# A graph layer's edge pass: picks of v and bf16 parts written with two-tensor VectorE operations

## The chip, the cores and the metric

The kernel runs on one core of a Trainium2 chip. The metric is the device time of one execution in microseconds (us). A core has five engines that run side by side and meet only at semaphores: TensorE (PE, with its weight loads as PEld), VectorE (DVE), ScalarE (ACT), GpSimd (POOL) and SyncE (SP), which only starts DMAs here. SBUF is the on-chip memory of 128 partitions, PSUM the small memory that PE writes to.

## The reference

A message passing layer over 6250 nodes with 64 features and 100000 edges (src, dst), the edges sorted by dst. `basis` holds 8 numbers for each edge.

```python
h = jnp.maximum(_layernorm(x, axis=-1), 0.0)
p1 = jnp.tanh(p @ pp_W1 + pp_b1) @ pp_W2 + pp_b2        # p = h
inter = jnp.concatenate([p1[idx_i], p1[idx_j]], axis=-1)  # idx_i = src, idx_j = dst
inter = inter @ pi_W1 + pi_b1
inter = inter @ pi_W2 + pi_b2
inter = inter @ pi_W3
inter = inter.reshape(inter.shape[0], D, N_BASIS)
i1 = jnp.einsum('ecb,eb->ec', inter, basis)
i1 = jnp.tanh(i1 @ ii_W1 + ii_b1) @ ii_W2 + ii_b2
out = jax.ops.segment_sum(i1, idx_j, num_segments=p1.shape[0])
return x + out
```

## The kernel before

A first stage of some 65 us works on the nodes. It normalises x, applies the first layers and multiplies the weights that stand between the gather and the einsum into each other, so that an edge needs only a row u[src] and a row v[dst] and their sum. The rows go to two tables in DRAM: `u_tab` in fp32, `v_tab` as three bf16 parts whose sum is the value.

The main stage goes over 391 groups of 512 edges (four tiles of 128, `TILES`, `GE`). Each engine has its own program, with the steps of successive groups interleaved: in step n, DVE works for groups n−4 to n+1. The order is written out by hand, and the engines meet at counting semaphores.

- POOL (L444 to L457) gathers the u rows: for each group four indirect DMAs (L453) with 128 rows each. An indirect DMA reads its 128 row numbers from `src_e` in SBUF. `u_rows` has UR = 8 buffers, so POOL waits (`s_ready`) only for the group eight before.
- SP (L367 to L391) brings for each group `loc_bc`, the place of each of the 512 destinations within a window of W = 42 nodes, spread to 126 partitions, and `v_win`, the window's 42 rows of v in three parts.
- DVE makes from them the pick `hot_t` (L834, `pick_t`): a bf16 0/1 matrix, 126 x 512, that is 1 where the place of the edge is the partition's number in `iota_p`. PE multiplies `v_win` by it (L1101, `sum_v`) and so picks the row of v of each edge, and adds the gathered rows of u in the same PSUM bank by a product with the identity (L1109, `place_rows`), which sets `s_ready`.
- ACT copies the sum to `st_sb` (L601). PE spreads the basis numbers over the features (L1118). DVE multiplies the two (L769, `products`, from SBUF and PSUM into `o_sb`), PE contracts (L1126), ACT takes tanh (L589), PE turns the result (L1133), ACT copies (L592), PE sums by destination (L1193) with the 0/1 matrix `hot` that DVE makes at L887 from two SBUF tensors, and DVE adds the sums of the window to `acc_all` (L862).
- Every 16 groups (`PIECE`) DVE splits the basis numbers of the next 16 into three bf16 parts, in steps of their own: `split_first` (L795, a rounding copy from fp32 to bf16), `split_less` (L799, subtract), `split_second` (L804, a rounding copy of the rest) and `split_third` (L808, subtract). Each works on 128 x 512 elements, all in SBUF. Every four groups it transposes the parts (L817, `turn`).

DVE's order within a step is: L862, then in some steps one of the four split operations, then in every fourth step L817, then the pick L834 for group n+1, then L887 for group n−2, then L769 for group n−1. Before the loop, DVE makes the parts of the first piece and the first pick. `zero1` is a column of zeros, 128 x 1, fp32, and `iota_p` a column with each partition's number within its third of the 126, fp32.

In the listing, the `Else` branches are for destination lists that don't fit the windows; they are not taken with these inputs.

Of the kernel before, what the change touches and what calls it, by code (L numbers as in the profile page):

```python
# [8 lines left out]
def program(nc, x, src, dst, edge_attr, pp_W1, pp_b1, pp_W2, pp_b2, pi_W1, pi_b1, pi_W2, pi_b2, pi_W3,  # L9
            ii_W1, ii_b1, ii_W2, ii_b2, out, u_tab, v_tab, loc_tab):  # L10
    f32, i32, u32, bf16 = mybir.dt.float32, mybir.dt.int32, mybir.dt.uint32, mybir.dt.bfloat16
    ALU, ACT, AX = mybir.AluOpType, mybir.ActivationFunctionType, mybir.AxisListType

    N, D = x.shape
    E, NB = edge_attr.shape
    P = 128
# [16 lines left out]
    TILES = 4  # L33
    GE = P * TILES
# [5 lines left out]
    W = P // 3  # L40
# [9 lines left out]
    VR = 4  # L50
# [24 lines left out]
    with ctx:  # L75
        def sb(name, shape, dt=f32):
            return ctx.enter_context(nc.sbuf_tensor(name, shape, dt))

        def sem(name):
            return ctx.enter_context(nc.semaphore(name))  # L80
# [16 lines left out]
        iota_p = sb("iota_p", [P, 3])  # L97
# [10 lines left out]
        loc_bc = sb("loc_bc", [P, VR, GE], bf16)  # L108
        hot_t = sb("hot_t", [3 * W, 2, GE], bf16)
# [36 lines left out]
        zero1 = sb("zero1", [P, 1])  # L146
# [68 lines left out]
        part1 = sem("part1_")  # L215
        part1r = sem("part1r")
        part2 = sem("part2_")
        part3 = sem("part3_")
        loc_ready = sem("loc_ready")
        hot_t_ready = sem("hot_t_ready")  # L220
# [41 lines left out]
        def ld_count(k):  # L262

            return 32 * (k // LD + 1)
# [369 lines left out]
        def _(dve):  # L634
# [141 lines left out]
            def span_of(k):  # L776
                return min(PIECE, NG - k * PIECE)

            def parts_of(k):
                return b_parts[:, k % 2 * PIECE:k % 2 * PIECE + span_of(k), :, :]  # L780

            def rest_of(k):
                return b_rest[:, 0:span_of(k), :, :]

            def basis_of(k):
                return basis[:, k * PIECE * NBT:(k * PIECE + span_of(k)) * NBT].rearrange(
                    "p (g t b) -> p g t b", t=TILES, b=NB)

            def split_first(k):
                dve.wait_ge(ld[k % LD], ld_count(k))  # L790
                if k == PIECES - 1:
                    dve.wait_ge(last_in, 32)
                if k >= 2:
                    dve.wait_ge(turned, (k - 1) * (PIECE // BT))
                nc.vector.tensor_copy(parts_of(k)[:, :, :, 0:NB], basis_of(k)).then_inc(part1, 1)  # L795

            def split_less(k):
                dve.wait_ge(part1, k + 1)
# [2 lines left out]

            def split_second(k):
                dve.wait_ge(part1r, k + 1)
                nc.vector.tensor_copy(parts_of(k)[:, :, :, NB:2 * NB], rest_of(k)).then_inc(part2, 1)  # L804

            def split_third(k):
                dve.wait_ge(part2, k + 1)
# [22 lines left out]
            def pick_t(g):  # L830
                dve.wait_ge(loc_in[g % VR], 16 * (g // VR + 1))
                if g >= 2:
                    dve.wait_ge(s_ready, g - 1)
                nc.vector.tensor_scalar(hot_t[:, g % 2, :], loc_bc[0:3 * W, g % VR, :], iota_p[0:3 * W, 0:1], None,  # L834
                                        ALU.is_equal).then_inc(hot_t_ready, 1)

            def add_early(b):
                cols = slice(slices_of(b).start * D, slices_of(b).stop * D)
# [3 lines left out]

            with dve.If(is_fast):
                split_first(0)
                split_less(0)
                split_second(0)
                split_third(0)
                turn(0)
                places()
                pick_t(0)  # L850
                for n in STEPS:
                    if n == 4:
                        dve.wait_ge(acc_zero, 1)
                    if has(n - 4):
                        g = n - 4
# [11 lines left out]
                    k = n // PIECE + 1  # L867
                    if k < PIECES:
                        if n % PIECE == 6:
                            split_first(k)  # L870
                        if n % PIECE == 8:
                            split_less(k)
                        if n % PIECE == 10:
                            split_second(k)
                        if n % PIECE == 12:
                            split_third(k)
                    if n % BT == 2 and has(n + 2):
                        turn((n + 2) // BT)
                    if has(n + 1):
                        pick_t(n + 1)  # L880
                    if has(n - 2):
                        g = n - 2
# [9 lines left out]
                    if has(n - 1):  # L892
                        g = n - 1
# [370 lines left out]
```

## Time and profile before

| | us |
|---|---|
| median of 3 runs | 2033.84 |
| lowest and highest of them | 2032.79, 2038.43 |
| the profiled execution | 2041.94 |
| its span in the trace | 2039.9 |

| engine | busy us | share of the span | instructions |
|---|---|---|---|
| PE | 1756.2 | 86% | 19956 |
| PEld | 1145.7 | 56% | 19956 |
| DVE | 1325.6 | 65% | 1894 |
| ACT | 1099.3 | 54% | 2401 |
| POOL | 1506.6 | 74% | 1582 |

All rows come from the one profiled execution; its own time is 2041.94 us, a little above the three others. A group row gives an operation's line, engine, name, the tile written and the tiles read, the shapes, its count, its busy time and mean, and the idle time of the engine just before such instructions with what ended most of it. "issue" is idle time in which the engine waited for nothing that the profile shows. In the timeline a row is an instruction or several alike: start, duration, engine, line, operation, tiles. The starts of two DVE instructions that follow each other directly overlap by some 0.08 us in these records.

### The profile page before, as it was taken

The numbers are of one execution on the slowest core, as the hardware profiler recorded it, in microseconds if no ns is written. First come the engines' busy times: TensorE is split into PE (matmuls) and PEld (weight loads), VectorE is DVE, ScalarE is ACT, GpSimd is POOL, SyncE is SP. The second block draws the span as 40 slices with busy tenths as digits, with TensorE's granted clock in tenths as the row PEclk, the third lists the DMA queues.
The fourth block names the chain that finished last, engine by engine and source line by source line (L and its number), as shares of the span: only waits on it lengthen the run. The fifth ranks groups of instructions, "written<-read, shape, count | busy, mean of one in ns | idle before, by whom it ended". The sixth has DMA issues, their size and how long they took to land.

```text
span 2039.9 us, 54797 instructions
## 1 busy us (share of the span) xinstructions
PE 1756.2 (86%) x19956; PEld 1145.7 (56%) x19956; DVE 1325.6 (65%) x1894; ACT 1099.3 (54%) x2401; POOL 1506.6 (74%) x1582
## 2 busy tenths in 40 slices
PE   5698888888889888888888988989888888888988
PEld 4465555555555555555555555555555555555765
DVE  6676666666666666666666666666666666666665
ACT  4565555555555555555555555555555555555554
POOL 2777777777777777777777777777777777777774
PEclk9799999999999999999999999899999998998999
DMA  5533233222332332322323323323233233222231
GB/s 124 132 68 62 54 62 61 56 60 55 60 61 55 61 62 55 63 58 58 60 55 60 61 55 62 60 55 61 55 61 60 55 60 61 55 57 55 58 73 40
DMA packets 261682, 126.82 MB, mean 62 GB/s; under 512 B 183545, under 2 KB 233704, under 8 KB 261432
## 3 DMA queue, kind: packets, MB, share of 16 engines
q1 hardware_dynamic: 210915, 74.15, 17.1%
q0 software_dynamic: 50048, 51.35, 12.8%
q14 instruction: 102, 0.84, 0.1%
q8 instruction: 23, 0.38, 0.1%
q10 hardware_dynamic: 594, 0.10, 0.0%
HBM read 119.47 MB, written 6.00 MB: 62 GB/s over the span
## 4 chain that ended last, share of the span: by engine, by line
POOL 68%; issue 22%; PE 6%; DMA 2%; DVE 1%; SPq 1%; ACT 0%; DVEq 0%; ACTq 0%; POOLq 0%
POOL u_rows L453 68%; PE bank L1126 3%; PE bank L1109 1%; DMA u_rows<-u_tab,src_e 1%; PE bank L1193 1%; PE bank L1133 0%; PE spread_ps L1118 0%; DMA x_sb<-x 0%; DMA v_tab<-acc_all 0%; PE bank L1101 0%; PE spread_ps L988 0%; PE spread_ps L976 0%; ACT loc_rows L557 0%; SPq L340 0%; DMA loc_bc<-loc_tab 0%
## 5 line engine op out<-in xcount | busy, mean ns | idle before, releaser
L453 POOL DMA_INDIRECT u_rows<-u_tab,src_e x1564 | 1500.1, 959 | 509.2 <-issue 474.5
L769 DVE TENSOR_TENSOR o_sb<-st_sb,spread_ps 128x2048 f32<-128x2048 f32 x391 | 894.1, 2287 | 488.9 <-PE spread_ps L1118 485.5
L601 ACT ACTIVATE st_sb<-bank,s_bias 64x256 f32<-64x256 f32 x1564 | 734.2, 469 | 473.8 <-PE bank L1109 457.3
L1126 PE MATMUL bank<-o_sb,g_sb 128*64 128x256 f32 x6256 | 837.7, 414 | 0.8 <-ACT t_sb L592 0.8
L1126 PEld LDWEIGHTS bank<-o_sb,g_sb 128*64 128x64 f32 x6256 | 444.4, 146 | 243.7 <-issue 55.9
L1109 PE MATMUL bank<-ident,u_rows 128*128 128x128 f32 x1564 | 285.6, 306 | 231.1 <-DMA u_rows<-u_tab,src_e 230.2
L1109 PEld LDWEIGHTS bank<-ident,u_rows 128*128 128x128 f32 x1564 | 209.2, 194 | 279.4 <-DMA u_rows<-u_tab,src_e 258.7
L1193 PEld LDWEIGHTS bank<-hot,t_sb 128*65 128x65 f32 x3128 | 225.3, 144 | 158.2 <-issue 155.9
L589 ACT ACTIVATE tt_sb<-bank,z_bias 128x256 f32<-128x256 f32 x391 | 185.5, 474 | 204.5 <-PE bank L1126 204.5
L1193 PE MATMUL bank<-hot,t_sb 128*65 128x42 f32 x3128 | 272.6, 240 | 0.5 <-ACT t_sb L592 0.5
L592 ACT COPY t_sb<-bank 128x256 f32<-128x256 f32 x391 | 146.8, 376 | 221.1 <-PE bank L1133 221.1
L862 DVE TENSOR_TENSOR acc_all<-acc_all,bank 65x42 f32 x391 | 76.4, 195 | 189.0 <-PE bank L1193 184.4
L1133 PE MATMUL bank<-ident,tt_sb 128*128 128x128 f32 x782 | 172.5, 303 | 0.6 <-ACT tt_sb L589 0.6
L1118 PE MATMUL spread_ps<-bt_sb,spread 24*128 24x128 bf16 x6256 | 162.1, 222 | 0.6 <-DVE o_sb L769 0.6
L834 DVE TENSOR_SCALAR hot_t<-loc_bc,iota_p 126x512 bf16<-126x512 bf16 x391 | 141.0, 361 | 10.8 <-DMA loc_bc<-loc_tab 9.4
L1101 PE MATMUL bank<-hot_t,v_win 126*64 126x128 bf16 x1564 | 118.6, 231 | 23.6 <-DVE hot_t L834 15.4
L887 DVE TENSOR_TENSOR hot<-loc_e,iota_f 128x168 f32<-128x168 f32 x391 | 126.9, 325 | 0.1
L1118 PEld LDWEIGHTS spread_ps<-bt_sb,spread 24*128 24x128 bf16 x6256 | 93.0, 94 | 49.7 <-issue 4.0
L1101 PEld LDWEIGHTS bank<-hot_t,v_win 126*64 126x64 bf16 x1564 | 55.5, 108 | 92.8 <-issue 90.8
L1133 PEld LDWEIGHTS bank<-ident,tt_sb 128*128 128x128 f32 x782 | 82.9, 147 | 33.9 <-ACT tt_sb L589 1.4
L817 DVE STREAM_TRANSPOSE bt_sb<-b_parts 128x512 bf16<-128x512 bf16 x98 | 68.8, 702 | 0.3 <-issue 0.3
L1141 PEld LDWEIGHTS bank<-w_out,acc_all 65*64 65x64 f32 (+1 forms) x160 | 15.9, 247 | 2.0 <-issue 0.4
(111 smaller groups left out, 223.2 us busy)
## 6 DMA issues: line engine op xcount, KB each, us to landing
loc_bc<-loc_tab SPq DMA_DIRECT2D x391, 126.0 KB
u_rows<-u_tab,src_e POOLq DMA_INDIRECT x1564
v_win<-v_tab SPq DMA_DIRECT2D x391, 15.8 KB
basis<-edge_attr SPq DMA_DIRECT2D x24, 256.0 KB, 4.0
v_tab<-acc_all SPq DMA_DIRECT2D x6, 336.0 KB
u_tab<-basis SPq DMA_DIRECT2D x6, 224.0 KB
x_sb<-x SPq DMA_DIRECT2D x1, 1120.0 KB
out<-x_sb SPq DMA_DIRECT2D x1, 784.0 KB
```

The source lines that it names most:

```text
L453: pool.indirect_dma_start(out=u_rows[:, g % UR, j, :], out_offset=None, in_=u_tab[:, :], in_offset=bass.IndirectOffsetOnAxis(ap=src_e[:, g ...
L589: return nc.scalar.activation(tt_sb[:, r, :], z_ps, ACT.Tanh, bias=z_bias[:, 0:1])
L592: return nc.scalar.copy(t_sb[:, r, :, 0:D].rearrange("p (h q) c -> p q h c", h=2), t_ps.rearrange("p (q h c) -> p q h c", q=2, h=2))
L601: last = nc.scalar.activation(tiles[h * D:(h + 1) * D, j], s_ps[r][part].rearrange("p (q a e) -> p q a e", q=2, a=TILES), ACT.Identity, bi ...
L769: return nc.vector.tensor_tensor(o_sb[:, r, :, :].rearrange("p c (j e) -> p j c e", j=TILES), st_sb[:, r, :].rearrange("p (j e) -> p j e", ...
L834: nc.vector.tensor_scalar(hot_t[:, g % 2, :], loc_bc[0:3 * W, g % VR, :], iota_p[0:3 * W, 0:1], None, ALU.is_equal).then_inc(hot_t_ready, 1)
L1101: nc.tensor.matmul(s_ps[u % 2][TWICE[j], q * P:(q + 1) * P].rearrange("k (a e) -> k a e", a=TILES), v_win[:, u % VR, :], hot_t[:, u % 2, : ...
L1109: last = nc.tensor.matmul(s_ps[r][:, q * P:(q + 1) * P], rows[:, 2 * q:2 * q + 2, :].rearrange("p j k -> p (j k)"), ident[:], start=alone ...
L1118: last = nc.tensor.matmul(spread_ps[:, a, c * P:(c + 1) * P], spread[q, 2 * c:2 * c + 2, :].rearrange("p b k -> p (b k)"), bt_sb[q, r, :], ...
L1126: last = nc.tensor.matmul(z_ps[h * D:(h + 1) * D, 0:2 * P], g_sb[:, c, :], o_sb[:, r, c, 2 * h * P:(2 * h + 2) * P], start=(c == 0), stop= ...
L1133: last = nc.tensor.transpose(t_ps[:, q * P:(q + 1) * P], tt_sb[:, r, q * P:(q + 1) * P], ident[:])
L1193: last = nc.tensor.matmul(seg_ps, t_sb[:, (u - 3) % 2, j, :], hot[:, (u - 3) % HR, j, :], start=(j == 0), stop=(j == TILES - 1))
```

## The change

The pick, L834, is a comparison of a tensor with a column as a per-partition scalar (`tensor_scalar`). It becomes a comparison of two tensors, the second being the same column repeated along the 512 elements (`tensor_tensor`). The two rounding copies of the split, L795 and L804, become sums of the same input with the column `zero1` repeated over its elements, written to the same bf16 places. Values, shapes, semaphores and the order of the work stay as they are. The copy in the branch that isn't taken stays too.

```diff
--- before.py
+++ after.py
@@ -786,13 +786,18 @@
                 return basis[:, k * PIECE * NBT:(k * PIECE + span_of(k)) * NBT].rearrange(
                     "p (g t b) -> p g t b", t=TILES, b=NB)
 
+            def rounded(to, of, n):
+
+                zero = zero1[:, 0:1].unsqueeze(2).unsqueeze(3).to_broadcast([P, n, TILES, NB])
+                return nc.vector.tensor_tensor(to, of, zero, ALU.add)
+
             def split_first(k):
                 dve.wait_ge(ld[k % LD], ld_count(k))
                 if k == PIECES - 1:
                     dve.wait_ge(last_in, 32)
                 if k >= 2:
                     dve.wait_ge(turned, (k - 1) * (PIECE // BT))
-                nc.vector.tensor_copy(parts_of(k)[:, :, :, 0:NB], basis_of(k)).then_inc(part1, 1)
+                rounded(parts_of(k)[:, :, :, 0:NB], basis_of(k), span_of(k)).then_inc(part1, 1)
 
             def split_less(k):
                 dve.wait_ge(part1, k + 1)
@@ -801,7 +806,7 @@
 
             def split_second(k):
                 dve.wait_ge(part1r, k + 1)
-                nc.vector.tensor_copy(parts_of(k)[:, :, :, NB:2 * NB], rest_of(k)).then_inc(part2, 1)
+                rounded(parts_of(k)[:, :, :, NB:2 * NB], rest_of(k), span_of(k)).then_inc(part2, 1)
 
             def split_third(k):
                 dve.wait_ge(part2, k + 1)
@@ -831,8 +836,9 @@
                 dve.wait_ge(loc_in[g % VR], 16 * (g // VR + 1))
                 if g >= 2:
                     dve.wait_ge(s_ready, g - 1)
-                nc.vector.tensor_scalar(hot_t[:, g % 2, :], loc_bc[0:3 * W, g % VR, :], iota_p[0:3 * W, 0:1], None,
-                                        ALU.is_equal).then_inc(hot_t_ready, 1)
+                nc.vector.tensor_tensor(hot_t[:, g % 2, :], loc_bc[0:3 * W, g % VR, :],
+                                        iota_p[0:3 * W, 0:1].to_broadcast([3 * W, GE]), ALU.is_equal
+                                        ).then_inc(hot_t_ready, 1)
 
             def add_early(b):
                 cols = slice(slices_of(b).start * D, slices_of(b).stop * D)
```

## Rows read from the trace of the kernel before

**Rows 1.** The page: busy time of each engine; the chain that ended last.

```profile
PE 1756.2 (86%) x19956; PEld 1145.7 (56%) x19956; DVE 1325.6 (65%) x1894; ACT 1099.3 (54%) x2401; POOL 1506.6 (74%) x1582
...
POOL 68%; issue 22%; PE 6%; DMA 2%; DVE 1%; SPq 1%; ACT 0%; DVEq 0%; ACTq 0%; POOLq 0%
POOL u_rows L453 68%; PE bank L1126 3%; PE bank L1109 1%; DMA u_rows<-u_tab,src_e 1%; PE bank L1193 1%; PE bank L1133 0%; PE spread_ps L1118 0%; DMA x_sb<-x 0%; DMA v_tab<-acc_all 0%; PE bank L1101 0%; PE spread_ps L988 0%; PE spread_ps L976 0%; ACT loc_rows L557 0%; SPq L340 0%; DMA loc_bc<-loc_tab 0%
```

**Rows 2.** Line L453: the page's row, then durations and what POOL idled for.

```profile
L453 POOL DMA_INDIRECT u_rows<-u_tab,src_e x1564 | 1500.1, 959 | 509.2 <-issue 474.5
...
L453 POOL DMA_INDIRECT u_rows<-u_tab,src_e x1564: 941/947/1528, 40.2 to 2016.0; - x196
...
  issue: 474.5, 1556
...
  PE bank L1109: 2.1, 7
```

**Rows 3.** The page: L769 and L834; then from the waits: PE for the gather.

```profile
L769 DVE TENSOR_TENSOR o_sb<-st_sb,spread_ps 128x2048 f32<-128x2048 f32 x391 | 894.1, 2287 | 488.9 <-PE spread_ps L1118 485.5
L834 DVE TENSOR_SCALAR hot_t<-loc_bc,iota_p 126x512 bf16<-126x512 bf16 x391 | 141.0, 361 | 10.8 <-DMA loc_bc<-loc_tab 9.4
...
PE bank L1109 <- DMA u_rows<-u_tab,src_e: 230.2, 152, 2.9
```

**Rows 4.** Timeline, DVE and POOL: start us, us, engine, line, operation, tiles, idle before.

```profile
998.83 2.29 DVE L769 TENSOR_TENSOR o_sb<-st_sb,spread_ps 128x2048 f32<-128x2048 f32 x1 [0.87 <-PE spread_ps L1118]
999.83 0.94 POOL L453 DMA_INDIRECT u_rows<-u_tab,src_e  x1 [0.30 <-issue]
1001.08 0.95 POOL L453 DMA_INDIRECT u_rows<-u_tab,src_e  x1 [0.31 <-issue]
```

**Rows 5.** Timeline, POOL and DVE, from 410.5 us.

```profile
410.59 1.53 POOL L453 DMA_INDIRECT u_rows<-u_tab,src_e  x1 [0.30 <-issue]
410.62 0.68 DVE L799 TENSOR_TENSOR b_rest<-basis,b_parts 128x512 f32<-128x512 f32 x1
```

**Rows 6.** Timeline, POOL and DVE, from 1228.1 us.

```profile
1228.11 1.26 POOL L453 DMA_INDIRECT u_rows<-u_tab,src_e  x1 [0.30 <-issue]
1228.14 0.42 DVE L804 CAST b_parts<-b_rest 128x512 bf16<-128x512 f32 x1
```

**Rows 7.** Timeline, DVE and POOL, from 152.9 us.

```profile
152.98 0.35 DVE L834 TENSOR_SCALAR hot_t<-loc_bc,iota_p 126x512 bf16<-126x512 bf16 x1
153.10 1.05 POOL L453 DMA_INDIRECT u_rows<-u_tab,src_e  x1 [0.31 <-issue]
```

**Rows 8.** Timeline, DVE and POOL, from 800.3 us.

```profile
800.32 0.33 DVE L887 TENSOR_TENSOR hot<-loc_e,iota_f 128x168 f32<-128x168 f32 x1
800.35 1.12 POOL L453 DMA_INDIRECT u_rows<-u_tab,src_e  x1 [0.30 <-issue]
```

**Rows 9.** Timeline, DVE and POOL, from 1403.1 us.

```profile
1403.17 0.68 DVE L808 TENSOR_TENSOR b_parts<-b_rest,b_parts 128x512 bf16<-128x512 f32 x1
1403.77 0.34 DVE L834 TENSOR_SCALAR hot_t<-loc_bc,iota_p 126x512 bf16<-126x512 bf16 x1
1403.81 1.37 POOL L453 DMA_INDIRECT u_rows<-u_tab,src_e  x1 [0.30 <-issue]
1404.03 0.32 DVE L887 TENSOR_TENSOR hot<-loc_e,iota_f 128x168 f32<-128x168 f32 x1
```

**Rows 10.** Timeline, DVE and POOL, from 835.2 us.

```profile
835.28 0.68 DVE L808 TENSOR_TENSOR b_parts<-b_rest,b_parts 128x512 bf16<-128x512 f32 x1
835.78 1.00 POOL L453 DMA_INDIRECT u_rows<-u_tab,src_e  x1 [0.30 <-issue]
```

**Rows 11.** Groups by shape, DVE: columns as on the page.

```profile
L799 DVE TENSOR_TENSOR b_rest<-basis,b_parts 128x512 f32<-128x512 f32 x24 | 16.4, 681 | 0.0
```

**Rows 12.** Timeline, PE, the rows of u placed by two successive groups.

```profile
83.17 0.71 PE L1109 MATMUL bank<-ident,u_rows 128*128 128x128 f32 x4
...
87.27 0.71 PE L1109 MATMUL bank<-ident,u_rows 128*128 128x128 f32 x4
```

## The prediction

> **What bounds the kernel now.** I read the page first, then the group rows, then the order of time around single instructions, because the change touches small VectorE operations and the question is whom they hold up. PE is busiest by share, 86%, but the chain that ended last runs 68% on POOL's line L453 and 22% in "issue", the pause between two POOL instructions [rows 1]. L453 is the gather of rows of u: 1564 indirect DMAs, four for each of the 391 groups [rows 2]. POOL's idle time before them is almost all "issue" (1556 times, 474.5 of 509.2 us), and the waits for PE are 2.1 us [rows 2]; the rest is one wait before the first gather. So POOL never really waits for a consumer: it goes from the first gather at 40.2 us to the last at 2016.0 us without a stop, and the other engines follow it. PE waits for u_rows 152 times, 230.2 us, and VectorE sits idle 488.9 us before its big product L769 [rows 3]. That is the cover of VectorE: 1.25 us a group.
>
> An undisturbed gather takes 0.95 us and starts 1.25 us after the one before [rows 4]. 1563 steps of 1.25 us are 1954 us; the trace has 2016.0 − 40.2 = 1975.8 us. So about 20 us are lost in gathers that take longer. The same number comes from the group: 1500.1 us busy less 1564 × 0.947 us (the median) is 19.0 us, with single gathers up to 1.53 us [rows 2]. I looked for what runs beside the long ones.
>
> **What a VectorE instruction does to a gather.** At 410.59 us the gather took 1.53 us: L799, a tensor_tensor whose two inputs both lie in SBUF, ran from 410.62 for 0.68 us, to 410.59 + 0.71. The excess is 1.53 − 0.95 = 0.58 us, which is L799's end less 0.13 us [rows 5]. At 1228.11 the cast L804 ended 0.45 us after the gather's start and the gather was 0.31 us too long: its end less 0.14 [rows 6]. At 153.10 the pick of v, L834, ended 0.23 after the start and the excess was 0.10 [rows 7]. At 800.35 it was L887, again a tensor_tensor from two SBUF tensors: end at 0.30, excess 0.17 [rows 8]. So each of these four kinds holds the gather back, if it runs at the gather's start, until the operation's end; the gather then goes on, 0.13 us of its own being done. Work with one input in PSUM does not show this: L769 runs over gather starts in every group, and those gathers take 0.94 to 0.95 us, as the two at 999.83 and 1001.08 [rows 4]. Whether the operation is a one-input cast or a two-input tensor_tensor decides nothing; its length does.
>
> **A price per operation.** If an operation of length d can catch a start from its own first moment up to 0.13 us before its end, and starts fall every 1.25 us at any phase, its mean cost is w²/2/1.25 with w = d − 0.10 (casts, L799, L808: the latest that still caught a gather began 0.03 us after it [rows 5, 6]). The pick must wait for two semaphores and gets hold later; of picks with no split operation ahead of them I found none that caught a gather after beginning less than 0.06 us before it, so w = d − 0.20. L887 has w of 0.16. Checked against the trace of now: L834, d 0.35: 0.009 × 391 = 3.5 us; L887: 0.010 × 391 = 4.0; the 50 casts, d 0.42: 0.041 × 50 = 2.0; L799 and L808, d 0.68: 0.135 × 49 = 6.6. Sum 16 us against the 19 to 20 measured. The rest is a second kind: at 1403.81 the gather was 0.42 us too long with L834 ending at 0.30 and L887 at 0.54, that is L887's end less 0.12. Behind the long L808 both were ready, and L887 went ahead of the waiting gather [rows 9]. The opposite is there too: at 835.78 the excess was only 0.05, L808's end at 0.18 less 0.13, and the gather slipped in ahead of L834 [rows 10].
>
> **The change, part by part.** It moves nothing: the same instructions stand in the same order on every engine, with the same waits.
>
> (a) The pick, 391 times, becomes a tensor_tensor of 512 elements a partition, bf16 against an fp32 column spread with step 0. The nearest row is L799, a 128x512 tensor_tensor of mixed types, 681 ns; L834 is 361 ns [rows 3, 11]. VectorE gets 391 × 0.32 = 125 us more work. All of it lies in the 488.9 us of cover; if the cover were gone it would cost its 125 us. Who waits for the pick: behind it on VectorE L887 and L769, on PE sum_v of the next group. PE can make a step in 4.10 us when rows are there (83.17 to 87.27 [rows 12]) while POOL needs 1975.8 / 391 = 5.05 us a group, so 0.3 us of lateness in a step is caught up. Cost on the path by time alone: 0.
> By holding gathers: w grows from 0.15 to 0.48; 0.48²/2.5 = 0.092 us × 391 = 36 us, less the 3.5 of now: +32.5 us.
>
> (b) The first halves of the split: 50 casts of 0.42 us [rows 6] become sums of 0.68 us. VectorE +12 us, under the same cover. Holding: 0.135 × 50 = 6.7, less 2.0: +4.7 us.
>
> (c) L887 right behind the longer pick. In a 0.68 us pick there is time to get L887 ready, and both are now the same kind of operation. If L887 always waits its turn behind the gather, as L834 did at 835.78, nothing is added. If it goes ahead as at 1403.81 once the pick has run 0.25 us, a gather caught in the later part waits for L887's end, 0.25 us more: (0.21 × 0.375 + 0.52²/2)/1.25 = 0.171 us a group for both, against 0.092 + 0.012 = 0.104 apart; +26 us, and up to some 12 us more behind the 49 operations L799 and L808. Bounds 0 and +38. I take +21, near the middle, because the two rows that bear on it point opposite ways.
>
> Sum: 32.5 + 4.7 + 21 = +58 us. Each microsecond here is on POOL's own chain and nothing can hide it. The tail after the last gather has no picks; the prologue has two casts more of 0.25 us while POOL already runs ahead: 0.
>
> Here a rule of the Trainium skill stands against my reading. "SBUF — State Buffer", section "Who interferes with whom", says that copies, casts and tensor_scalar can take two port pairs and then lock GpSimd out fully, while tensor_tensor has no such mode, touches only GpSimd's reads, and did not stall DMAs in their probe because descriptor writing needs the write side (marked as inferred there). By it the change would give back what the picks and casts cost, a sum of −8 us in place of +58. The trace disagrees in the point that matters: the longest gather of all, 1.53 us, stood beside a tensor_tensor [rows 5].
>
> **Against the runs.** The profiled execution took 2041.94 us (span 2039.9), the median of the three is 2033.84 us. The sum is a difference against that execution; phases alone can move its 20 us by several, so I add it to the median: 2033.84 + 58 = 2092 us.
>
> **The rivals.**
> *The new operations don't hold gathers (faster).* Then the 3.5 + 2.0 us, and the 3 us of the second kind, vanish: −8 us, 2026 us. It decides if a step-0 second input is not such a read. Against it: L887 has step-0 inputs and holds gathers [rows 8]. Chance 0.04.
> *The phases don't mix.* If VectorE's steps settle at a phase to the gathers, the pick could miss nearly all starts, costing some 0 to 6 us net (chance 0.03, no change), or hit most, at up to 0.48 us a group: far over +100. Now the picks fall at all phases, and PE's catching up in every second or third group stirs them. Most of it lies above the range (0.05 there), less of it between 2040 and 2052 us (0.04).
> *L887 never goes ahead*: +37 us, 2071. *It always does*, with the chains: +75, 2109. Both inside the forecast.
> *VectorE becomes the bound.* It needs 1325.6 + 137 = 1463 us of 2100, 3.7 us a group; it would have to pass 5.05 us a group. Under 0.01.
>
> **Numbers.** A measurement of this kernel tells 0.3%, 6 us, from no change. The forecast case runs from L887 never to L887 always ahead, 2071 to 2109 us. The rule gave 16 us where the trace had 20, so a quarter of its new total (16 + 58 − 21 = 53 at the one end, 91 at the other) may be luck of the phases: 2071 − 19 (the quarter of 53 and 6 us between the runs themselves) and 2109 + 23, which is 2052 to 2132 us. It has 0.84; slower but outside it 0.09; same 0.03; faster 0.04. So faster 0.04, same 0.03, slower 0.93, and the predicted time is 2092 us.
>
> **What would show it.** Right: the pick and the sums at 0.68 us; L453 still 1564 times with a median of 0.947 us but a mean of about 0.996 (0.959 + 58/1564), with hundreds of gathers of 1.1 to 1.7 us; POOL's idle time still "issue"; VectorE near 1463 us busy and L769's idle time down by some 80 us. Wrong: if the mean stays at 0.96 or falls, two-input picks hold nothing and step (a) falls; if POOL starts to wait for L1109, the cover was too thin; if the mean is over 1.03, the phases lock.

## The result, and the profile after

The changed kernel takes 2101.32 us (median of 4 runs, 2099.01 to 2109.22), the kernel before 2036.13 us in its 4 runs. The ratio is 1.0322, with a 95% interval of 1.0305 to 1.0339: slower by 65 us.

The page of the kernel after, its engines, its chain and the four groups that matter. L839 is now the pick (before L834), L893 the making of `hot` (before L887), L868 the adding of the window (before L862), L804 and L813 the two subtractions of the split (before L799 and L808), and L792 the new sum with zero.

```profile
PE 1775.3 (85%) x19956; PEld 1156.6 (55%) x19956; DVE 1456.5 (69%) x1894; ACT 1100.3 (52%) x2401; POOL 1565.5 (75%) x1582
...
POOL 72%; issue 22%; PE 3%; DMA 1%; DVE 0%; SPq 0%; DVEq 0%; ACT 0%; POOLq 0%
...
L453 POOL DMA_INDIRECT u_rows<-u_tab,src_e x1564 | 1559.0, 997 | 510.6 <-issue 474.8
L769 DVE TENSOR_TENSOR o_sb<-st_sb,spread_ps 128x2048 f32<-128x2048 f32 x391 | 893.9, 2286 | 417.9 <-PE spread_ps L1124 406.9
...
L839 DVE TENSOR_TENSOR hot_t<-loc_bc,iota_p 126x512 bf16<-126x512 bf16 x391 | 263.9, 675 | 10.2 <-DMA loc_bc<-loc_tab 8.9
L893 DVE TENSOR_TENSOR hot<-loc_e,iota_f 128x168 f32<-128x168 f32 x391 | 127.3, 325 | 0.0
```

Against [rows 1 to 3], POOL is busy 58.9 us longer, 1559.0 in L453 after 1500.1, and the span has grown by 59.4 (2099.3 after 2039.9). L453's mean went from 959 to 997 ns at the same count of 1564. The time in which POOL stood before L453 is the same, 510.6 after 509.2, and again "issue". So the whole loss lies inside the gathers. VectorE works 131 us more and has 71 us less idle time before L769; that its longer work cost nothing by itself is shown by f3 below.

The timeline of the kernel after around its longest gather:

```profile
839.65 0.20 DVE L868 TENSOR_TENSOR acc_all<-acc_all,bank 65x42 f32 x1 [0.24 <-PE bank L1199]
839.74 2.38 POOL L453 DMA_INDIRECT u_rows<-u_tab,src_e  x1 [0.30 <-issue]
839.77 0.68 DVE L804 TENSOR_TENSOR b_rest<-basis,b_parts 128x512 f32<-128x512 f32 x1
840.37 0.68 DVE L839 TENSOR_TENSOR hot_t<-loc_bc,iota_p 126x512 bf16<-126x512 bf16 x1
840.97 0.32 DVE L893 TENSOR_TENSOR hot<-loc_e,iota_f 128x168 f32<-128x168 f32 x1
```

The subtraction began 0.03 us after the gather; the pick and L893 followed without a gap, until 840.97 + 0.32 = 841.29, which is 1.55 us after the gather's start. The gather took 2.38 us, 1.43 too long: the end of the third operation less 0.12. In [rows 5], with the same subtraction at the same place but a pick with a scalar, the gather went on behind the first operation.

The same over the whole traces, for the gathers that began during a subtraction with a pick directly behind it, while more than 0.14 us of the subtraction was left: before, 20 of 20 were released at the subtraction's own end; after, 21 of 22 only at the end of L893, the third operation.

I sorted all gathers of over 0.967 us by the operation whose end, less 0.13 us, gives their excess over 0.947 ("released by" that operation):

| released by | before: gathers, us | after: gathers, us |
|---|---|---|
| the pick | 28, 1.9 | 100, 26.0 |
| `hot`, L887 or L893 | 57, 7.7 | 111, 51.0 |
| the two subtractions of the split | 20, 6.8 | 1, 0.1 |
| the copies, then the sums | 15, 2.6 | 23, 4.6 |
| all, with the rest | 127, 20.4 | 237, 82.2 |

The sum of all grew by 61.8 us, which is the loss within the runs' spread. The 111 gathers released by L893 are of three sorts, by what VectorE was in when the gather began and what stood directly before it:

| released by L893 | gathers | us | of it, up to the pick's end | up to the subtraction's end |
|---|---|---|---|---|
| alone: the pick was over, or had under 0.13 us to go | 53 | 6.3 | | |
| in a pick that follows no subtraction | 13 | 7.9 | 4.7 | |
| in a subtraction (21) or in the pick directly behind it (24) | 45 | 36.9 | 25.8 | 6.2 |

In the trace 48 picks stand directly behind a subtraction, so 45 gathers beside these 48 places bear 36.9 of the 82.2 us.

### The profile page after: what moved, and what is told of

Same layout as the page of the kernel before. It is cut to its first block, busy times and chain, and to the rows that moved or that the text cites. A ratio compares the mean times of both kernels' runs of the same rounds, so it can differ in the third digit from the quotient of the medians.

```text
span 2099.3 us, 54797 instructions
## 1 busy us (share of the span) xinstructions
PE 1775.3 (85%) x19956; PEld 1156.6 (55%) x19956; DVE 1456.5 (69%) x1894; ACT 1100.3 (52%) x2401; POOL 1565.5 (75%) x1582
## 4 chain that ended last, share of the span: by engine, by line
POOL 72%; issue 22%; PE 3%; DMA 1%; DVE 0%; SPq 0%; DVEq 0%; ACT 0%; POOLq 0%
POOL u_rows L453 72%; PE bank L1132 1%; DMA u_rows<-u_tab,src_e 1%; PE bank L1115 0%; DMA x_sb<-x 0%; PE bank L1199 0%; PE spread_ps L994 0%; PE spread_ps L982 0%; PE spread_ps L1147 0%; PE spread_ps L1124 0%; DVE basis L676 0%; PE bank L1139 0%; PE bank L1000 0%; DVE rowst L714 0%; DVEq L710 0%
## 5 line engine op out<-in xcount | busy, mean ns | idle before, releaser
L453 POOL DMA_INDIRECT u_rows<-u_tab,src_e x1564 | 1559.0, 997 | 510.6 <-issue 474.8
L769 DVE TENSOR_TENSOR o_sb<-st_sb,spread_ps 128x2048 f32<-128x2048 f32 x391 | 893.9, 2286 | 417.9 <-PE spread_ps L1124 406.9
L1115 PE MATMUL bank<-ident,u_rows 128*128 128x128 f32 x1564 | 293.2, 313 | 268.3 <-DMA u_rows<-u_tab,src_e 266.8
L1115 PEld LDWEIGHTS bank<-ident,u_rows 128*128 128x128 f32 x1564 | 215.2, 199 | 318.9 <-DMA u_rows<-u_tab,src_e 301.4
L839 DVE TENSOR_TENSOR hot_t<-loc_bc,iota_p 126x512 bf16<-126x512 bf16 x391 | 263.9, 675 | 10.2 <-DMA loc_bc<-loc_tab 8.9
L868 DVE TENSOR_TENSOR acc_all<-acc_all,bank 65x42 f32 x391 | 76.1, 195 | 186.5 <-PE bank L1199 180.2
L893 DVE TENSOR_TENSOR hot<-loc_e,iota_f 128x168 f32<-128x168 f32 x391 | 127.3, 325 | 0.0
L822 DVE STREAM_TRANSPOSE bt_sb<-b_parts 128x512 bf16<-128x512 bf16 x98 | 68.8, 703 | 0.3 <-issue 0.3
```

The source lines that it names most:

```text
L453: pool.indirect_dma_start(out=u_rows[:, g % UR, j, :], out_offset=None, in_=u_tab[:, :], in_offset=bass.IndirectOffsetOnAxis(ap=src_e[:, g ...
L769: return nc.vector.tensor_tensor(o_sb[:, r, :, :].rearrange("p c (j e) -> p j c e", j=TILES), st_sb[:, r, :].rearrange("p (j e) -> p j e", ...
L839: nc.vector.tensor_tensor(hot_t[:, g % 2, :], loc_bc[0:3 * W, g % VR, :], iota_p[0:3 * W, 0:1].to_broadcast([3 * W, GE]), ALU.is_equal).th ...
L1115: last = nc.tensor.matmul(s_ps[r][:, q * P:(q + 1) * P], rows[:, 2 * q:2 * q + 2, :].rearrange("p j k -> p (j k)"), ident[:], start=alone ...
```

## The experiments

The theories: **A**, a gather that begins while VectorE runs an operation reading a second tensor from SBUF (or one of the one-input copies and comparisons, 0.42 and 0.35 us for their 512 elements) waits for its end, so the length and the place of the operands decide; **B**, the loss is VectorE's longer work, which makes groups late; **C**, any tensor_tensor holds a gather, wherever it reads.

Three chips were used. The first four kernels (e1 to e4) ran on one on which the kernel before took 2538.74 us. Three of them were run again as f1, f3 and f4, with e6, on a second, where it took 2038.57 us, and the fourth as f2, with e5 and e8, on a third, where it took 2040.03 us. Each ratio is against the kernel before on the same chip.

**e1_pick_only and f1_pick_only.** The kernel before with the new pick alone:

```diff
-                nc.vector.tensor_scalar(hot_t[:, g % 2, :], loc_bc[0:3 * W, g % VR, :], iota_p[0:3 * W, 0:1], None,
-                                        ALU.is_equal).then_inc(hot_t_ready, 1)
+                nc.vector.tensor_tensor(hot_t[:, g % 2, :], loc_bc[0:3 * W, g % VR, :],
+                                        iota_p[0:3 * W, 0:1].to_broadcast([3 * W, GE]), ALU.is_equal
+                                        ).then_inc(hot_t_ready, 1)
```

> Only the pick is a comparison of two tensors; the rounding copies stay copies. Theory A (a gather that starts beside a VectorE operation reading through its second SBUF input, or a two-sided copy, waits for that operation's end, so length decides): nearly the whole loss, +50 to +62 us, 2086 to 2098 us, VectorE about 1445 us busy, mean of L453 about 0.99 us. Theory B (the loss is VectorE's longer work making groups late): also nearly all of it, since 123 of the 131 us of added work are here. The run is for the share, not to tell A from B.

> The kernel of e1_pick_only again, for the same reason. Where the kernel before takes about 2036 us: theory A +50 to +62 us, 2086 to 2098 us; theory B also nearly the whole loss.

Measured on the first chip: 2618.35 us, ratio 1.0294 (1.0245 to 1.0342). POOL's longest wait before the gather in that run: what waited, for what, us, times, longest.

```profile
POOL u_rows L453 <- PE bank L1110: 513.2, 284, 5.8
```

POOL waited 513.2 us for PE's L1110, which adds the gathered rows: there the kernel is bound by PE (63% of its chain, mean granted clock 0.844), not by POOL. Neither theory was made for that case, and the first chip decides little between them.

Measured on the second: 2101.99 us, ratio 1.0308 (1.0278 to 1.0338), 63 us more than the kernel before, a little above the 50 to 62 expected. L453 has a mean of 997 ns, and its long gathers sum to 82.3 us, as with the whole change. The pick is nearly the whole loss; both theories had said so.

**e2_sums_only and f2_sums_only.** The change with the pick put back to `tensor_scalar`; only the sums with zero are new.

```diff
-                nc.vector.tensor_tensor(hot_t[:, g % 2, :], loc_bc[0:3 * W, g % VR, :],
-                                        iota_p[0:3 * W, 0:1].to_broadcast([3 * W, GE]), ALU.is_equal
-                                        ).then_inc(hot_t_ready, 1)
+                nc.vector.tensor_scalar(hot_t[:, g % 2, :], loc_bc[0:3 * W, g % VR, :], iota_p[0:3 * W, 0:1], None,
+                                        ALU.is_equal).then_inc(hot_t_ready, 1)
```

> Only the 50 rounding copies become sums with zero; the pick stays with its scalar. Theory A: +3 to +9 us (50 operations at 0.135 us a piece less 2 us for the copies, and picks behind them), 2039 to 2045 us. Theory B: +0 to +1 us, as 12 us more work in 391 groups lies in idle time.

> The kernel of e2_sums_only again where the kernel before takes about 2036 us: theory A +3 to +9 us, 2039 to 2045 us; theory B 0 to +1 us.

Measured: 2555.42 us on the first chip, ratio 1.0055 (1.003 to 1.0079); 2043.39 us on the third, ratio 1.0016 (1.0004 to 1.0029), +3.4 us. That is inside what A gave and above B's 0 to 1, but the interval, +0.8 to +5.9 us, reaches into both, so this run hardly decides between them. In the profiled execution the sums released 12 gathers, for 3.3 us; its total of 20.4 us is that of the kernel before, so a single execution does not show the difference.

**e3_second_in_psum and f3_second_in_psum.** The change with the repeated operands moved to PSUM (the zero of the first piece, before the loop, stays in SBUF). PE waits one pick longer before it writes to that bank.

```diff
+        col_ps, zero_ps = bank[7][:, W:W + 1], bank[7][:, W + 1:W + 2]
...
-                zero = zero1[:, 0:1].unsqueeze(2).unsqueeze(3).to_broadcast([P, n, TILES, NB])
+                zero = (zero_ps if k else zero1)[:, 0:1].unsqueeze(2).unsqueeze(3).to_broadcast([P, span_of(k), TILES, NB])
...
-                                        iota_p[0:3 * W, 0:1].to_broadcast([3 * W, GE]), ALU.is_equal
+                                        col_ps[0:3 * W, :].to_broadcast([3 * W, GE]), ALU.is_equal
...
                 places()
+                dve.drain()
+                nc.vector.tensor_copy(col_ps, iota_p[:, 0:1])
+                nc.vector.tensor_copy(zero_ps, zero1[:, 0:1])
+                dve.drain()
                 pick_t(0)
...
-                    pe.wait_ge(hot_ready, seen(3))
+                    pe.wait_ge(hot_ready, min(NG, seen(3, 1)) if last_pass else seen(3, 1))
```

> As the change, but the repeated column of the pick and the zero of the sums lie in PSUM, in free columns of bank 7; PE's sum by destination waits for the pick's step, so that the two do not use the bank at once. The operations stay as long (0.68 to 0.75 us), VectorE is as busy as in the change or more (1450 to 1490 us). Theory A: the holds of the pick and of the sums are gone, with those of the copies: 2022 to 2034 us, under the kernel before. Theory B: as slow as the change or slower, 2095 to 2110 us. Theory C (any tensor_tensor holds a gather, wherever it reads): as the change too.

> The kernel of e3_second_in_psum again, since in that call the kernel before itself took 2538.74 us at a mean granted clock of about 0.86, with PE on 63 to 70% of the chain, and so was bound otherwise. Where the kernel before takes about 2036 us: theory A 2022 to 2034 us with VectorE 1450 to 1490 us busy; theory B and theory C 2095 to 2110 us.

Measured: 2564.35 us on the first chip, ratio 1.01 (1.0062 to 1.0138). On the second 2029.96 us, ratio 0.9954 (0.9936 to 0.9972), under the kernel before. Its page, the engines, L454 (the gather) and L840 (the pick):

```profile
PE 1746.3 (86%) x19956; PEld 1139.2 (56%) x19956; DVE 1454.3 (72%) x1896; ACT 1097.5 (54%) x2401; POOL 1491.6 (74%) x1582
...
L454 POOL DMA_INDIRECT u_rows<-u_tab,src_e x1564 | 1485.1, 950 | 508.8 <-issue 476.1
...
L840 DVE TENSOR_TENSOR hot_t<-loc_bc,bank 126x512 bf16<-126x512 bf16 x391 | 261.8, 670 | 9.3 <-DMA loc_bc<-loc_tab 8.8
```

VectorE is as busy as in the change (1454.3 against 1456.5 us), the pick as long (670 against 675 ns), and it is the same tensor_tensor; only the second operand's place differs. The ratio falls from 1.0322 to 0.9954, and the time is 72 us below f1's on the same chip. B and C fall. Here a gather beside a pick in each of the two kernels, first the change, then this one:

```profile
984.13 0.68 DVE L839 TENSOR_TENSOR hot_t<-loc_bc,iota_p 126x512 bf16<-126x512 bf16 x1
984.29 1.33 POOL L453 DMA_INDIRECT u_rows<-u_tab,src_e  x1 [0.30 <-issue]
```

```profile
1145.98 0.68 DVE L840 TENSOR_TENSOR hot_t<-loc_bc,bank 126x512 bf16<-126x512 bf16 x1
1146.13 0.94 POOL L454 DMA_INDIRECT u_rows<-u_tab,src_e  x1 [0.30 <-issue]
```

The pick began 0.16 and 0.15 us before the gather, and ran on beside it for half a microsecond. The one gather took 1.33 us, the other 0.94. Over the whole trace, the gathers that began 0.05 to 0.5 us after a pick had a mean of 1.30 us in the change (125 of them) and of 0.94 us here (128). Of those that began with more than 0.22 us of the pick left, all 113 were held to its end in the change and none of 109 here.

**e4_bf16_pair and f4_bf16_pair.** The kernel before with a new pick alone; the rounding copies stay copies. The pick is a tensor_tensor from SBUF, but a shorter one: it compares with `iota_w`, the column written out once as 126 x 512 in bf16.

```diff
+        iota_w = sb("iota_w", [3 * W, GE], bf16)
...
-                nc.vector.tensor_scalar(hot_t[:, g % 2, :], loc_bc[0:3 * W, g % VR, :], iota_p[0:3 * W, 0:1], None,
-                                        ALU.is_equal).then_inc(hot_t_ready, 1)
+                nc.vector.tensor_tensor(hot_t[:, g % 2, :], loc_bc[0:3 * W, g % VR, :],
+                                        iota_w[:, :], ALU.is_equal
+                                        ).then_inc(hot_t_ready, 1)
...
+                nc.vector.tensor_copy(iota_w[:, :], iota_p[0:3 * W, 0:1].to_broadcast([3 * W, GE]))
+                dve.drain()
```

> The pick compares two bf16 tensors in SBUF, the second written out once as 126 x 512 with step 1; copies stay copies. If it runs at two elements a cycle it takes about 0.42 us instead of 0.68. Theory A: the price goes with the square of the length: (0.42 - 0.20) squared / 2.5 = 0.019 us a group against 0.009 for the scalar form, and with L887 behind it some more: +2 to +15 us, 2038 to 2051 us. Theory C (the kind decides, not the length): near e1, 2085 us or more. If the pick stays at 0.68 us, both say as e1.

> The kernel of e4_bf16_pair again. Its pick takes 0.408 us. In the other call its mean L453 was about 0.975 us against 1.009 of the pick alone at 0.673 us and 0.965 of the sums alone, so the gathers lose some 0.016 to 0.02 us a piece more than before, 25 to 30 us in all, more than the 2 to 15 of the first expectation: 2045 to 2065 us by theory A with L887 ahead of the waiting gather; theory C 2085 us or more.

Measured: 2581.76 us on the first chip, ratio 1.0174 (1.0116 to 1.0231); 2050.91 us on the second, ratio 1.0058 (1.0041 to 1.0075), +12.3 us. The time lies inside both expectations of theory A, 2038 to 2051 and 2045 to 2065 us. Groups of the profile on the second chip:

```profile
L454 POOL DMA_INDIRECT u_rows<-u_tab,src_e x1564 | 1508.3, 964 | 509.9 <-issue 475.8
...
L835 DVE TENSOR_TENSOR hot_t<-loc_bc,iota_w 126x512 bf16<-126x512 bf16 x391 | 159.7, 408 | 10.2 <-DMA loc_bc<-loc_tab 8.9
```

At 408 ns instead of 674 the pick costs a fifth of what it costs in f1. So the length decides, as A says, but not by the square alone: (0.41 − 0.20)²/2.5 × 391 is 6.9 us against the 3.5 of the scalar form, +3.4, and it was +12.3. In its trace 77 gathers with 22.8 us were released by L891, which is `hot`; 57 with 7.7 us were before.

Here the traces show something that theory A leaves out. Of the gathers that began in a subtraction directly before a pick, with more than 0.14 us of it left, 15 of 18 in f4 waited for the whole row up to the end of `hot`, as did 28 of 28 in f1. With the pick as a `tensor_scalar` all were released at the subtraction's own end (20 of 20 before, 30 of 30 in f2), and so they were with the pick's second operand in PSUM (12 of 12 in f3). The pick of f4 is only 0.05 us longer than the scalar form. So length sets what one operation costs, but whether a gather gets in between two operations goes by whether the next one also reads two tensors from SBUF.

**e5_hot_row_psum.** The change, with the pick and the sums in SBUF, and the row of `hot` in PSUM. To make room the sums of the early nodes go in batches of six.

```diff
+        row_ps = bank[7][:, D:D + W]
-        y_area = bank[7][0:NP, D:D + SLICE * D]
+        y_area = bank[7][0:NP, 2 * D:2 * D + SLICE * D]
...
-                            iota_f[:, 0:W].unsqueeze(1).to_broadcast([P, TILES, W]),
+                            row_ps.unsqueeze(1).to_broadcast([P, TILES, W]),
...
-    SLICE = 7
+    SLICE = 6
...
+                nc.vector.tensor_copy(row_ps, iota_f[:, 0:W])
...
-                    pe.wait_ge(hot_ready, seen(3))
+                    pe.wait_ge(hot_ready, min(NG, seen(3, 1)) if last_pass else seen(3, 1))
```

> The change with its two-input pick and sums, but the row that L887 compares with lies in PSUM. In the trace of the change 111 gathers were released by the end of L887: 53 of them by L887 alone (6.3 us), 58 from behind a pick, where L887 going ahead added 14.3 us to what the pick had cost. Theory A: both go, -18 to -24 us against the change, 2077 to 2086 us where the change takes 2101 to 2102. If L887's part is bound up with the pick's length alone, only the 6 us: 2095.

Measured: 2093.44 us, ratio 1.0266 (1.0245 to 1.0288) against its kernel before of 2040.03; the change stands at 1.0322. Neither figure was met: it lies below the 2095 of the one reading and above the 2077 to 2086 of the other. In its trace no gather is released by `hot` any more, and the sum of the long ones is 67.7 us instead of 82.2. But the pick releases 160 gathers for 59.9 us, and 46 of them, for 29 us, began in a subtraction or in the pick directly behind it: two operations in a row are still a row. What `hot` costs can't be subtracted by itself.

**e6_all_psum.** The operands of f3 and the row of e5 in PSUM together: to the diff of e5 it adds

```diff
-                zero = zero1[:, 0:1].unsqueeze(2).unsqueeze(3).to_broadcast([P, n, TILES, NB])
+                zero = (zero_ps if k else zero1)[:, 0:1].unsqueeze(2).unsqueeze(3).to_broadcast([P, span_of(k), TILES, NB])
...
-                                        iota_p[0:3 * W, 0:1].to_broadcast([3 * W, GE]), ALU.is_equal
+                                        col_ps[0:3 * W, :].to_broadcast([3 * W, GE]), ALU.is_equal
```

> As e3, and the row that L887 compares with lies in PSUM too (the sums for the early nodes go in batches of six instead of seven to make room). Only L799 and L808 still read two SBUF tensors. Theory A: also the 4 us of L887 and what it added behind others go: 2018 to 2030 us, at the floor of 1564 gathers at 1.25 us plus 84 us around them, 2039, less what lies between the profiled run and the median, 6 us, and some 8 us of L799 and L808. Theory B: 2095 us or more.

Measured: 2024.92 us, ratio 0.9934 (0.9917 to 0.9951), 13.6 us under the kernel before, and inside theory A's 2018 to 2030. Its page, the gather's group and the pick's:

```profile
L455 POOL DMA_INDIRECT u_rows<-u_tab,src_e x1564 | 1482.8, 948 | 510.0 <-issue 476.0
...
L841 DVE TENSOR_TENSOR hot_t<-loc_bc,bank 126x512 bf16<-126x512 bf16 x391 | 261.8, 670 | 8.9 <-DMA loc_bc<-loc_tab 8.1
```

The long gathers sum to 6.5 us, 5.3 of them beside the two subtractions, which still read SBUF twice. This is the fastest kernel of the study, with VectorE 127 us busier than in the kernel before.

**e8_pick_scalar_rest_psum.** As e6, but the pick is the `tensor_scalar` of before:

```diff
-                nc.vector.tensor_tensor(hot_t[:, g % 2, :], loc_bc[0:3 * W, g % VR, :],
-                                        col_ps[0:3 * W, :].to_broadcast([3 * W, GE]), ALU.is_equal
-                                        ).then_inc(hot_t_ready, 1)
+                nc.vector.tensor_scalar(hot_t[:, g % 2, :], loc_bc[0:3 * W, g % VR, :], iota_p[0:3 * W, 0:1], None,
+                                        ALU.is_equal).then_inc(hot_t_ready, 1)
```

> The pick stays a comparison with its scalar (0.35 us), the zero of the sums and the row of L887 lie in PSUM. VectorE is 120 us less busy than in e6_all_psum. Theory A: the holds of L887 and of the copies are gone, those of the pick (3.5 us), of L799 and L808 (7 us) stay: 2024 to 2031 us, 2 to 5 us over e6. If the length of VectorE's work mattered at all here (theory B), it would be under e6.

Measured: 2031.36 us, ratio 0.9951 (0.9932 to 0.997). VectorE has 1334.2 us of work instead of 1452.4, and the kernel is no faster than e6: the two intervals overlap, and the lower median is that of the busier VectorE. So B finds nothing here either. The time lies 0.4 us above the expected range. The pick released 22 gathers, 1.8 us, half of what I took for it. The long gathers sum to 5.9 us, about as in e6, so holds don't explain the distance between the two. Of the 6.5 us between the profiled spans, 2.6 lie in L453 (1485.4 us against 1482.8; a gather that nothing holds has a median of 947 ns here and 944 there) and most of the rest behind the last gather. The two ran on different chips, and why they differ so is open.

## Why the prediction was right, and where it was off

The forecast was 2092 us in a range of 2052 to 2132; measured were 2101.32, +65 us where it had +58. The mechanism held; two terms of the sum were mis-sized in opposite directions, so that the sum came this near is in part luck.

- **What bounds the kernel** held: POOL's chain went from 68% to 72%, its idle time stayed "issue", and the loss is the growth of L453 to a mean of 997 ns (forecast 996), at a median of 944. Not foreseen was the length of the worst: 159 gathers took more than 1.1 us, but 22 of them more than the 1.7 us named, up to 2.38.
- **Time on VectorE is covered** held: 1456.5 us busy (1463 forecast), and f3 shows the same work at no cost.
- **(a) The pick** is right where it follows no subtraction: 100 + 13 gathers, 26.0 + 4.7 = 30.7 us, against 36 × 343/391 = 31.6 by the rule. For the 48 picks directly behind a subtraction the same price makes 4.4 us, and this is the term that was mis-sized most: they cost 25.8 − 6.2 = 19.6 us, 15 more. The step that failed priced every operation by itself, with a gather let in between. The trace before had already shown L887 going ahead of a waiting gather [rows 9]. With the new pick, a gather that began in the subtraction waited for the whole row in 21 of 22 cases; the one exception stood at the short last piece.
- **(b) The sums** cost 3.4 us in f2 by themselves (4.7 forecast), with an interval of 0.8 to 5.9.
- **(c) `hot` going ahead** cost 14.3 us, 3.2 behind a pick alone and 11.1 behind a subtraction, where I took 21 between 0 and 38: 7 too much, which made up for half of what (a) had too little. When it goes ahead can be read in part from what stood before the pick (of the gathers that began up to 0.5 us after a pick's start). Directly behind a subtraction L893 went ahead 23 times of 23, and 18 of 18 in f1. Where VectorE had idled for PE before L868, it never did in 73 cases. Where it had worked up to L868 without a gap, L893 went ahead 13 times of 14. Behind the transpose L822 it never did, 17 times. In f1 the gapless case gave 4 of 16 and the transpose 4 of 31, so these two are a tendency at best, and the mechanism is open. A gapless case in the kernel after:

```profile
95.97 2.28 DVE L769 TENSOR_TENSOR o_sb<-st_sb,spread_ps 128x2048 f32<-128x2048 f32 x1
98.16 0.19 DVE L868 TENSOR_TENSOR acc_all<-acc_all,bank 65x42 f32 x1
98.27 0.68 DVE L839 TENSOR_TENSOR hot_t<-loc_bc,iota_p 126x512 bf16<-126x512 bf16 x1
98.42 1.60 POOL L453 DMA_INDIRECT u_rows<-u_tab,src_e  x1 [0.30 <-issue]
98.87 0.32 DVE L893 TENSOR_TENSOR hot<-loc_e,iota_f 128x168 f32<-128x168 f32 x1
```

The pick ended 0.53 us after the gather's start and L893 0.77; the excess was 0.65.

- **The rivals.** That the new operations would hold nothing was refuted by f1 and f3 together. The rule of the Trainium skill ("SBUF — State Buffer", section "Who interferes with whom") has two halves. That a tensor_tensor with both inputs in SBUF meets GpSimd's reads agrees with f1 against f3: 63 us slower with the second input in SBUF, 9 us faster with it in PSUM. Its inference, that descriptor generation is spared by it, doesn't fit: the gathers that begin inside such a pick take 1.30 us instead of 0.94, with the place of its second input as the difference. Whether it is the reading of the row numbers that waits, no run here shows.
- VectorE as the bound did not come up on the chips where POOL bounds the kernel.
- **Slips in the working.** The upper end of the range, 2109 + 23, leaves out the 6 us between runs that the lower end has; with them it would be 2138. Of the two gathers shown for L769 the one at 1001.08 began 0.04 us before L769's end, too late to be held by the rule anyway. The other bears the reading out, and the rest of the trace does too: of the 624 gathers that began in L769 of the kernel before with at least 0.4 us of it left, none took more than 0.96 us. And that a one-input cast or a two-input operation "decides nothing" holds for one operation's hold, not for a row of them.

Open: why the kernel before took 2538.74 us on the first chip, and why the pick cost 2.9% there as well, where POOL waits for PE. The gathers were held there too: L453 was busy for 1578.0 us in e1 and for 1490.2 in e3, 88 us less, while the times are 54 us apart. On that chip e3 was slower than the kernel before (1.01) and on the second faster (0.9954), so what the longer operations cost VectorE's own users may count there. That is not shown.

## What to carry to other kernels

When GpSimd issues gathers back to back and is the chain, look at the duration of each gather beside what VectorE runs at its start, not at shares of busy time: two-input operations from SBUF and short one-input copies on VectorE were paid for there, by their length, and the two-input ones as one when several stood in a row. Replacing the one-input pick (361 ns) by a two-input one (675 ns) made the hold longer; putting the second operand in PSUM removed it at equal length (f3, e6). If such operations must stay, break up rows of them: a `tensor_scalar`, or a two-input operation with one operand in PSUM, behind a subtraction let the gather in (62 of 62 in the kernel before, f2 and f3). It pays where the gathers are the bound; on the first chip, where PE was, e3 was no gain.

## What the runs showed that I had not expected

- Three two-input operations in a row held one gather for 1.43 us; with the `tensor_scalar` in their middle no gather of the kernel before was held for more than 0.58 us.
- The second operand of a comparison in PSUM cost VectorE nothing: 670 ns against 675 from SBUF, and 317 against 325 for `hot` in e6.
- A comparison of two bf16 tensors with step 1 took 408 ns for 512 elements a partition, against 675 with the column repeated, and 361 for the form with a scalar.
- The same kernel before took 2036 us on one chip and 2539 us on another. TensorE's mean granted clock was 0.84 to 0.86 in the profiled executions of e1 to e4, on that chip, against 0.92 to 0.94 in the others.
